# Dense products for the first 512 destination nodes in layers 1 and 2 of a three-layer GNN with a feed-forward block

## The reference, cut to what matters

```python
N_NODES, N_EDGES, D = 12500, 200000, 256
src = randint(0, 12500)                                    # source of each edge
dst = (12500 * uniform() ** 2.0).astype(int32)             # destination, skewed to low nodes
src, dst = src[argsort(dst)], dst[argsort(dst)]

def _sage_layer(x, src, dst, inv_deg, W_self, W_neigh, b):
    agg = segment_sum(x[src], dst, num_segments=N_NODES)
    return x @ W_self + (agg * inv_deg[:, None]) @ W_neigh + b

inv_deg = 1.0 / maximum(segment_sum(ones, dst), 1.0)
h = relu(_sage_layer(layernorm(x), ...layer 0...))
h = relu(_sage_layer(h, ...layer 1...))
x = x + _sage_layer(h, ...layer 2...)
y = layernorm(x)                                           # 12500 rows, one batch
w = y @ wr + br                                            # a weight per row
sel = the 6249 rows of largest w
x = x + y;  x[sel] += w[sel] * (gelu(y[sel] @ w1 + b1) @ w2 + b2)
```

## Time and profile before

| | us |
|---|---|
| median of 3 runs (lowest, highest) | 6282.49 (6279.57, 6283.19) |
| the profiled execution, its own time | 6277.99 |
| its span, first to last instruction | 6276.2 |

### The profile page before, as it was taken

One profiled execution on the slowest core, in us unless ns is written; L12 is line 12 of the kernel. 1 busy time (PEld: TensorE's weight loads), 2 busy tenths in 40 slices (PEclk: granted clock), 3 DMA queues, 4 the chain that ended last, 5 costly groups with the idle time before them and its releaser, 6 DMA issues.

```text
span 6276.2 us, 96211 instructions
## 1 busy us (share of the span) xinstructions
PE 4104.0 (65%) x20011; PEld 2433.3 (39%) x20012; DVE 2259.7 (36%) x4900; ACT 946.2 (15%) x2227; POOL 4448.2 (71%) x4700
## 2 busy tenths in 40 slices
PE   0445656677778645555666676654566788899993
PEld 0222333344445322222223333322234556677772
DVE  7112223333444311122223334421223344555556
ACT  6000000111111100000000000100011223334440
POOL 0777777777777577777777777767777777777750
PEclk9677778888999866677777788866778899999996
DMA  7555555565666555555556666655555656666644
GB/s 246 158 158 160 163 165 166 168 170 170 173 174 175 148 158 158 163 164 165 167 168 170 171 173 175 176 147 159 161 164 165 168 170 170 175 175 176 178 136 167
DMA packets 459717, 1053.84 MB, mean 168 GB/s; under 512 B 127891, under 2 KB 234087, under 8 KB 459687
## 3 DMA queue, kind: packets, MB, share of 16 engines
q0 software_dynamic: 300288, 922.79, 52.5%
q10 hardware_dynamic: 82908, 97.60, 4.5%
q1 hardware_dynamic: 76491, 33.10, 2.0%
HBM read 969.11 MB, written 84.02 MB: 168 GB/s over the span
## 4 chain that ended last, share of the span: by engine, by line
POOL 47%; issue 19%; PE 19%; DMA 11%; DVE 2%; ACT 1%; POOLq 1%; DVEq 0%; SPq 0%; ACTq 0%
POOL gath L494 47%; DMA gath<-table,idx_ring 10%; PE agg L609 8%; PE agg L611 3%; PE y L664 2%; PE hid L654 2%; PE y L548 1%; DMA idx_ring<-idx_dram 1%; PE hid L548 0%; PE hid L611 0%; PE lo L611 0%; PE hid L573 0%; DMA resid<-x 0%; POOLq L490 0%; PE tp L535 0%
## 5 line engine op out<-in xcount | busy, mean ns | idle before, releaser
L494 POOL DMA_INDIRECT gath<-table,idx_ring x4692 | 4447.4, 948 | 1641.5 <-issue 1539.4
L609 PE MATMUL agg<-gath,onehot 128*128 x5856 | 2464.8, 450 | 2007.9 <-SPq L429 1815.4
L609 PEld LDWEIGHTS agg<-gath,onehot 128*128 x5856 | 633.7, 108 | 3086.4 <-issue 2776.8
L883 DVE TENSOR_TENSOR onehot<-ids_ps,dst_f 128x512 f32 x1464 | 1012.8, 692 | 1980.3 <-PE agg L611 1126.5
L611 PE MATMUL agg<-gath,onehot 128*128 x3904 | 1238.2, 317 | 0.0
L611 PEld LDWEIGHTS agg<-gath,onehot 128*128 x3904 | 424.1, 109 | 127.8
L914 DVE SCALAR_TENSOR_TENSOR resid<-agg,inv_deg,resid 128x256 f32 (+1 forms) x196 | 94.7, 483 | 863.8 <-PE agg L611 863.1
L664 PE MATMUL y<-w_sb,hidT 128*128 128x256 f32 x1568 | 378.0, 397 | 3.0 <-ACT hidT L1244 3.0
L654 PEld LDWEIGHTS hid<-featT,w_gnn 128*128 128x128 f32 x3136 | 365.9, 192 | 4.9
L654 PE MATMUL hid<-featT,w_gnn 128*128 128x128 f32 x3136 | 366.5, 275 | 0.0
L1131 ACT ACTIVATE featT<-tp 128x256 f32<-128x256 f32 x196 | 75.0, 383 | 1886.3 <-PE tp L535 1769.3
(11 more groups left out here) (136 smaller groups left out, 2750.8 us busy)
## 6 DMA issues: line engine op xcount, KB each, us to landing
gath<-table,idx_ring POOLq DMA_INDIRECT x4692
table<-split ACTq DMA_DIRECT2D x194, 192.0 KB
table<-gath ACTq DMA_DIRECT2D x24, 768.0 KB, 3.6
xb<-x ACTq DMA_DIRECT2D x97, 128.0 KB
yw_dram<-yw ACTq DMA_DIRECT2D x97, 128.0 KB, 2.9
resid<-x SPq DMA_DIRECT2D x24, 512.0 KB, 7.8
gath<-yw_dram SPq DMA_DIRECT2D x24, 512.0 KB, 8.8
out<-gath ACTq DMA_DIRECT2D x24, 512.0 KB, 9.0
```

Source lines behind the costliest of these rows:

```text
L494: g.indirect_dma_start(gath[:, j, 0:PARTS * D], None, table[layer][:, :], bass.IndirectOffsetOnAxis(ap=idx_ring[:, h, i:i + 1], axis=0)).t ...
L609: mm(agg[p][:, 0:2 * D], oh, tile_rows[:, :, 0:2 * D], start=False, **flags)
L883: v.tensor_tensor(onehot[:, bass.ds(pair, GROUP), :], window_ids[p].unsqueeze(1).to_broadcast([P, GROUP, P]), dst_f[:, bass.ds(tiles, GROU ...
```

## The change

1. **Ring.** RING goes from 32 slots to 16 (4 blocks); the index ring's halves go from 16 to 8 tiles.
2. **One-hots.** The tile `ids_ps` goes, and with it L872 and the PSUM operand; a block's one-hots are 4 `tensor_scalar` on SBUF (iota plus window base, compared with a destination; two per-partition scalars), each 128x128 fp32 in, bf16 out.
3. **Counting, in layer 0.** In slots 6 to 69, two groups of 4 nodes each per slot (128 groups, nodes 0 to 511), counts are made of how often each source node occurs: for each tile of the group DVE makes a one-hot of the source's low 7 bits (128x128) and one of (node, source's high bits) (128x400), PE multiplies them (bf16, 400 columns), ACT copies the group's 128x400 counts to `stage`, and after 8 groups ACT stores them (1.6 MB, pieces of 512 bytes). Each group reads its first and last tile with two register loads, on PE and on DVE. In slot 4 DVE and PE find the groups' tile limits (`split_sources`, `count_ends`).
4. **Dense products, in layers 1 and 2.** Windows 4 to 97 are gathered first, windows 0 to 3 come last. The gathers begin at turn t0 of the ring (16 tiles), the turn in which window 4 begins. In slots 6 to 30 PE multiplies the counts with the rows themselves in fp32: per slot 4 chunks of 128 nodes by 4 windows, 16 products of 128x128 by 128x256 (8 in slot 30). For each, ACT issues a load of 1 MB of counts and 0.5 MB of rows. Windows 0 to 3 then wait for `dense_done` and take one DVE operation each.
5. **Stores.** Layers 0 and 1 also keep fp32 rows: ACT copies 128x256 and stores 128 KB more per window.
6. **Moved.** The load of w2 goes from SP's queue before layer 0 to ACT's queue after it. The last batch buffers lie half in `gath`, half in the new tile `dense`. POOL makes two more iotas at the start and waits for `steps_ready` before it gathers.

The diff, cut to its core:

```diff
-RING = 32
+RING = 16
+DENSE = 4
+CHUNKS_PER_BLOCK = 4
+GROUP_NODES = 4
+COUNT_COLS = 100
+DENSE_AT = 6
+COUNT_AT = 6
+COUNT_RING = 4
...
+    COUNT_LOOPS = [(COUNT_AT, COUNT_END, 4), (COUNT_END, LAST_LOOPED, 2)]
+    DENSE_LOOPS = [(DENSE_AT, DENSE_LAST, 2), (CLEAN, LAST_LOOPED, 2)]
...
 def onehots(layer, n, half, p, part):
-                v.tensor_scalar(window_ids[p], iota_row[:], window_base[:, col(n)], None,
-                                ALU.add).then_inc(ids_ready, 1)
-                    dve.wait_ge(slots_free, b + (layer * PADDED_BLOCKS + 2))
-                    v.tensor_tensor(onehot[:, bass.ds(pair, GROUP), :],
...
+                    dve.wait_ge(slots_free, b + dve_base[layer])
+                    dve.sem_inc(dve_turn, 1)
+                    for j in range(GROUP):
+                        last = v.tensor_scalar(onehot[:, bass.ds(pair, GROUP), :][:, j, :], iota_row[:],
+                                               window_base[:, col(w)], dst_f[:, bass.ds(tiles, GROUP)][:, j:j + 1],
+                                               ALU.add, ALU.is_equal)
+                    last.then_inc(onehot_ready, 1)
...
+            def count_onehots(g):
+                lo, hi = dve_groups(g)
+                dve.wait_ge(count_copied, g + 1)
+                with dve.Fori(lo, hi + 1) as t:
+                    slot = dve.snap((t + g) % COUNT_RING)
+                    dve.wait_ge(count_used, t + 2)
+                    v.tensor_scalar(low_hots[:, bass.ds(slot, 1), :], iota_row[:].unsqueeze(1),
+                                    src_low[:, bass.ds(t, 1)], None, ALU.is_equal)
+                    v.tensor_scalar(key_hots[:, bass.ds(slot, 1), :], iota_keys.unsqueeze(1),
+                                    group_base[:, col(g)], src_key[:, bass.ds(t, 1)],
+                                    ALU.add, ALU.is_equal).then_inc(count_hots, 1)
...
+            def count_group(g):
+                lo, hi = pe_groups(g)
+                pe.wait_ge(count_copied, g + 2)
+                def count_tile(t, stop):
+                    pe.wait_ge(count_hots, t + g + 1)
+                    return mm(count_ps[:, 0:GROUP_NODES * COUNT_COLS], low_hots[:, bass.ds(slot, 1), :],
+                              key_hots[:, bass.ds(slot, 1), :], stop=stop, **flags)
...
+            def dense_block(layer, k, p, last_block=False):
...
+                for c in range(2 if last_block else CHUNKS_PER_BLOCK):
+                    for w in range(DENSE):
+                        last = mm(dense_ps[w], counts[p][0:r, w * P:(w + 1) * P, c], node_rows[p][0:r, c, :],
+                                  start=False, stop=ends, skip_group_check=True)
+                last.then_inc(dense_done, 1)
...
             def slot_ffn(w, half, p, part):
                 if exists(w - 2):
                     transposes(3, w - 2, p)
                 if exists(w - 4):
                     ffn_down(w - 4, p)
                 if exists(w - 3):
                     ffn_up(w - 3, 1 - p)
+                dense_step(2, w, p, part)
                 if exists(w):
-                    aggregate(2, w, half, p)
+                    aggregate(2, w, half, p, part)
...
+            def slot_layer0(w, half, p, part):       # DVE
+                if isinstance(w, int) and w == COUNT_AT - 2:
+                    split_sources()
+                if part and part[0] == 0:
+                    for j in range(2):
+                        count_onehots(part[1] * 8 + (part[2] * 2 + j))
                 if exists(w):
...
-                with pool.Fori(0, FULL_TURNS) as it:
+                with pool.Fori(t0 if layer else 0, FULL_TURNS) as it:
                     gather_turn(it, RING_BLOCKS)
...
+                y = product_ps(phase, p)[0:r, 0:D]
+                a.copy(y32[p][0:r, :], y)
+                a.copy(split[p][0:r, 0, :], y).then_inc(hi_ready, 1)
...
+                act.dma_start(window_rows(rows_f32[phase], w), y32[p][0:r, :]).then_inc(y32_stored[p], 16)
```

More of the change, by code:

```diff
@@ L304, in col, with half_of @@
             return bass.ds(n, 1) if not isinstance(n, int) else slice(n, n + 1)
+        def half_of(layer, half, part, w):
+            if isinstance(w, int):
+                return w // 2
+            return half + DENSE // 2 if layer and part[0] == 0 else half
         def window_rows(t, n):
@@ L433, in relay_turn @@
                                      ).then_inc(idx_loaded[h], 16)
-                with sp.Fori(0, FULL_TURNS) as it:
+                landed_base = [turns_left * (16 * GROUP * layer) + 16 * GROUP * (layer * more + 1) if layer else 16 * GROUP
+                               for more in range(2)]
+                with sp.Fori(t0 if layer else 0, FULL_TURNS) as it:
                     relay_turn(it, RING_BLOCKS)
@@ new lines, in aggregate @@
+            def aggregate(layer, n, half, p, part):
+                w = window_of(layer, n, part)
+                if not gathered(layer, w):
+                    pe.wait_ge(dense_done, layer * DENSE_BLOCKS)
+                    pe.wait_ge(agg_ready, layer * NT + n)
+                    pe.sem_inc(agg_ready, 1)
+                    return
+                first, shared = pe_blocks(half_of(layer, half, part, w), p)
+                if layer and isinstance(n, int) and n == 0:
+                    first = pe.snap(pe_t0 * RING_BLOCKS)
@@ L927, in slot_layer0 @@
+            def slot_layer0(w, half, p, part):
+                if isinstance(w, int) and w == COUNT_AT - 2:
+                    split_sources()
+                if part and part[0] == 0:
+                    for j in range(2):
+                        count_onehots(part[1] * 8 + (part[2] * 2 + j))
                 if exists(w):
-                    onehots(0, w, half, p)
+                    onehots(0, w, half, p, part)
                 if exists(w - 1):
@@ L1248, in _, with slot_ffn @@
             act.wait_ge(feat_ready, turned(2, NT - 1))
-            def slot_ffn(w, half, p):
+            for p in range(2):
+                act.wait_ge(y32_stored[p], 16 * NT)
+            def slot_ffn(w, half, p, part):
+                load_step(2, w, part)
                 if exists(w):
```

406 lines of the change are left out of this document (321 added, 85 removed).

## The result

The changed kernel takes **6478.26 us** (median of 4 runs, 6462.27 to 6484.52) where the kernel before took 6281.03 beside it: a ratio of 1.031, 95% interval 1.0291 to 1.033. The forecast was 5985 us in 5690 to 6200, so it has the sign wrong and the time 493 us too low. Numbers are therefore compared within a set, and the verdicts rest on the later three.)

The account below looks back on a forecast made before the run. POOL's issue of 4692 gathers was taken as the bound. From 6278 us, 761 saved and 210, 50 and 205 given back in layers 0, 1 and 2, plus 4.5 for the median, gave 5985, range 5690 to 6200.

Parts of the forecast that it names:

- The gain: Layers 1 and 2: 608 gathers not started, at 1.251 us each, save 761 us of POOL's time.
- Layer 0: Give-back of 210 us in the layer with the counting, between 60 and 330.
- DVE becomes the bound: Layer 0's counted slots: one-hots and control take DVE 17.7 us near n = 57, against 13.0 of gathers.
- The 14 us for stores of counts and 10 for the limits: Layer 0: copies waiting for count stores cost 14 us; finding tile limits in slot 4 leaves 10 not hidden.
- Layer 1: Give-back of 50 us: dense slots' heads 25, loads 15, dense windows at the end 10.
- Layer 2: Give-back of 205 us from dense slots, late windows, end heads and loads; 95 without DVE-PE coupling, 330 at worst.
- The dense windows: Windows 0 to 3, taken at the end of layers 1 and 2: four heads each, 10 and 30 us.
- How much the small ring hides: Four blocks hide about 13 us of PE's head (33 before); outside counted and dense slots POOL should not wait.
- The rule weighed: All layers: a skill's rule that two-port `tensor_scalar` blocks gathers; the forecast took nothing for it.
- rival C: All layers: new one-hots block and slow the gathers; 7630 us at full lock, 6535 at a third; chance 0.10.
- B: All layers: the small ring costs more, 330 + 80 + 330, giving 6260 us; chance 0.13.
- D: Layers 1 and 2: gathers are not skipped, the give-back stands alone, 6747 us; chance 0.01.

Follow-up runs that it names:

- h2: The changed kernel without any counting in layer 0's slots (tile list and stores stay): 0.9629 of the kernel before.
- g1: The changed kernel with VectorE's two one-hots of every counted tile left out: 1.0217 of the kernel before.
- h3: The changed kernel with the counting's shell alone (loops, register loads, waits, hand-overs): one-hots, copies, all but each group's last product left out; 1.0141 of the kernel before.
- i1: The changed kernel with six blocks of one-hots and fewer control instructions in the counting, every count made: 1.0116 of the kernel before.
- g4: The changed kernel with six blocks of one-hots beside the four of gathered rows, same results: 1.0076 of the kernel before.
- f4: The changed kernel counting 4 groups a slot in slots 6 to 37, not 2 in slots 6 to 69: 1.0216 of the kernel before.
- g3: The changed kernel with each counted slot's counting moved behind the window's aggregation, the window's one-hots made first: 1.0769 of the kernel before.

## Why the prediction was wrong, step by step

**The gain** held: 608 gathers not started, 4084 left. At one rate of 1.251 us that is the 761 us of the sum, and h2, which has the rest of the change, stands at 0.963.

**Layer 0 is the step that failed**, in two terms: the engine that was made the bound, and what the ring of four blocks was to hide. "DVE becomes the bound" was the heading, and the sum had 17.7 us of VectorE for a slot near n = 57. The slots there measure 18.3 us (mean of windows 53 to 60), and the 24 windows from 46 measure 118 us over before, where 108 were forecast. So the size came out near there by luck, since the engine was another: with VectorE's count one-hots away (g1) these slots still take 17.5, and with no counting 13.1, VectorE's pair one-hots and means untouched (108 busy us of 200 in the row of h2). Over slots 8 to 69 the counting takes 6.4 us a slot and lengthens it by 5.8, from 18.3 (h2) to 24.1, so all but 0.6 comes out at the end. TensorE's waits for gathered rows did give way, from 5.0 us a slot to 2.5, but its products took most of that back (L791 takes 506 ns on average where h2 has 434) and its waits for VectorE's one-hots grew by 0.8. In windows 46 to 69 TensorE waits for rows 0.2 us a slot (2.2 before): there the turn is TensorE's. Its counting section was priced in slots 6 to 9 alone, as the time in which it aggregates nothing. TensorE's loads, branches and hand-overs are in no row of before at this density, but VectorE's 0.85 us before L872 was a price for such control, and TensorE's sum of a slot should have had it as well.

Because of both terms the early slots were taken as free. By windows, extra time over before against the forecast:

| windows | forecast | measured | with the shell alone |
|---|---|---|---|
| to slot 4 | 10 | 16 | 20 |
| 5 to 9 | 35 | 98 | 71 |
| 10 to 17 | 0 | 70 | 48 |
| 18 to 29 | 5 | 74 | 51 |
| 30 to 45 | 38 | 79 | 56 |
| 46 to 69 | 108 | 118 | 87 |

The assumption was that a window with many tiles has gathers enough to cover a counting. TensorE does have time in such windows: in windows 10 to 17 it still waits 7.2 us a slot for rows, 8.5 before. But the ring doesn't let POOL run on while TensorE is at its head and its counting. The prediction took it that about 13 us of such a pause are hidden. The trace lets this be read in each slot: the pause is the time from the end of a window's last product to L778 of the next, the stop is POOL's idle time beyond the usual 0.31 us before a gather (us, means of a slot):

| changed kernel | pause | POOL's stop | hidden |
|---|---|---|---|
| layer 0, slot 6 | 47.5 | 41.5 | 6.0 |
| layer 0, 7 to 9 | 19.8 | 14.5 | 5.3 |
| layer 0, 10 to 17 | 14.0 | 8.8 | 5.2 |
| layer 0, 18 to 29 | 11.3 | 6.1 | 5.2 |
| layer 0, 30 to 45 | 10.4 | 4.8 | 5.6 |
| layer 0, 46 to 69 | 9.5 | 5.1 | 4.4 |
| layer 1, windows 10 to 18, 19 to 34 | 10.0, 9.9 | 5.5, 3.4 | 4.5, 6.5 |
| layer 2, windows 10 to 18, 19 to 34 | 15.6, 16.5 | 9.3, 7.9 | 6.3, 8.6 |

```profile
711.64 0.94 POOL L602 DMA_INDIRECT gath<-table,idx_ring  x1 [41.83 <-PE lo L793]
```

That is the stop of slot 6. Between 4 and 9 us are hidden, not 13, whatever makes the pause: in h3 5.8 of 12.1 in windows 10 to 17, in i1 5.1 of 14.8. This fits i1, which gained nothing: its section is shorter, but the pause is not (14.8 against g4's 14.3 in windows 10 to 17, 10.5 against 9.3 in 46 to 69). Twice the counting in half the slots (f4) gained nothing either, on the other chip. No run gave the counting a ring of eight blocks, so how much a deeper ring would hide is not shown. The 14 us for stores of counts and 10 for the limits have 36 in h2, near enough.

**Layer 1**, 50 forecast and 129 measured: no counting is in it. By stretches, POOL's stops are 59 us in windows 10 to 18, 49 in 19 to 34, 11 at the dense windows. The pause itself lies where it was forecast ("9 to 14 us: at the edge of 13"), 10.0 and 9.9 us; it is the 13 that was wrong, so that POOL stops in the dense slots. g4's ring takes 31 us of it.

**Layer 2**, 205 forecast, 399 measured. A dense slot's own products were sized well (7.3 us forecast, 7.5 measured from 5112.68 on), but windows 10 to 18 give 84 us for 22, windows 19 to 34 121 for 80 (27.3 us a slot where I had 24), the windows before them 18 for nothing, the late ones 130 (153 less the 23 of before) for 50. The mechanism of the late windows was the one I described, the fourth one-hot behind the block that TensorE frees, and g4 shows it: 99.5 us come back. Its size was off, 3.9 us a window of four pairs (18.25 against 14.35; 14.63 with g4's ring) where 2.3 were taken. I take it that this is TensorE's own wait for VectorE's chain, which I had left out there; g4 removes both at once.

**The dense windows** I had placed last, here and in the list of the change, four heads of 10 and 30 us. In fact slots 0 to 30 take windows 4 to 34, slots 31 to 34 the dense windows 0 to 3, and windows 35 to 97 come last. POOL then stops once, 46.5 us before 5396.94 in layer 2 and 11 in layer 1. The amount was near, the place wrong.

**How much the small ring hides** ("outside the counted and dense slots POOL should not wait") holds for layer 1 (no stop over 0.1 us after the dense slots and windows) and fails for late layer 2, where the pauses of 8 to 10 us and the late fourth one-hot stop POOL in windows 46 to 96 for 122 us.

**The rule weighed and rival C.** 5216 new pair one-hots and 890 of the count go with gathers of 956 ns where they were 948, which is 15, 10 and 11 us in the three layers, 36 in all or 0.006 us an operation, an eighth of what rival C needed. Taking nothing was right. The Trainium skill (SBUF — State Buffer, Who interferes with whom) has a full stop behind a `tensor_scalar` in a two-port mode; `tensor_tensor` has no such mode there, but contends with GpSimd's reads when both its inputs lie in SBUF. Here the kernel with `tensor_tensor` of 512 columns, both inputs in SBUF, has the longer gathers, 979 ns; whether GpSimd's reads are the reason, no run shows. With a full stop behind every `tensor_scalar` the changed kernel would have stood at 7630 us, and it does not.

**Rivals.** B was the nearest in kind (4-block ring dearer, 330 + 80 + 330), and at 6260 it, too, was 218 us short. The slower side had been given to C and D alone, and no rival had TensorE's counting as the bound or a ring that hides 5 us. That is where the range broke: it was built on bounds of a sum in which TensorE's counting was missing from slot 10 on, and the 13 us stood without a range.

## What to carry to other kernels

Price an addition on every engine that it touches, instructions that do no work among them. Small data-dependent loops cost about a microsecond for each entry here, on TensorE (0.91 to 1.23 us) as much as on VectorE (0.85), and on the engine that frees the buffers this is time of the bound. That an engine is busy 156 of 200 us doesn't say that the other 44 are free: of 6.4 us put into each slot of TensorE, 5.8 came out at its end. What a ring hides of a pause is not its depth: of four blocks, 20 us of gathers, 4 to 9 us were left. Read it as the consumer's pause less the producer's stop. When a ring is cut, look at who shares its depth; two blocks more of the cheap half (one-hots) were worth 150 of the 197 us of loss.

## What the runs showed that I had not expected

Moving the same instructions to another place of the slot cost 283 us (g3), far more than leaving any of them out brought, because ScalarE's order of work tied three engines into one chain. Leaving out ScalarE's 128 copies of 0.49 us brought nothing (2416.1 against 2406.2), though TensorE's next group is released by them. The counting costs TensorE time twice: products of the aggregation take 0.63 and 0.42 us after the counting and 0.38 and 0.27 later in the same slot, the lower and the higher level of its clock (1.2 and 2.4 GHz), and the mean of L791 in slots 8 to 69 is 506 ns with the counting and 434 without (granted clock in 1600 to 1800: 0.80 and 0.90). And four `tensor_scalar` of 360 ns, back to back, take 1.11 us as the timeline counts them, not 1.44.
